# Attention and gated feed-forward on one core: where the projection weights are split, and who adds the output projection

## The reference

```python
h = _layernorm(x) * (1 + ca) + sa
qkv = (h @ W_qkv + b_qkv).reshape(b, l, H, 3 * DK).transpose(0, 2, 1, 3)
Q, K, V = jnp.split(qkv, 3, axis=-1)
scores = jnp.einsum('bhqd,bhkd->bhqk', Q, K) / np.sqrt(DK)
out = jnp.einsum('bhqk,bhkv->bhqv', softmax(scores), V)
x = x + ga * (out.transpose(0, 2, 1, 3).reshape(b, l, H * DK) @ W_fc + b_fc)
```

## Time and profile before

| | us |
|---|---|
| median of 3 runs | 1827.69 |
| lowest and highest run | 1825.25 and 1830.28 |
| the profiled execution, and its span | 1822.86 and 1821.4 |
| PE busy | 1644.4 (90%) |
| DVE busy | 1345.1 (74%) |
| POOL busy | 1130.2 (62%) |
| ACT busy | 829.1 (46%) |
| DMA queue 1 | 6.2% of 16 engines' span |

### The profile page before, as it was taken

The page is one execution under the profiler, slowest core; times in us unless marked ns, Lnnn a source line. Parts: engine busy times, 40 slices in busy tenths (PEclk is TensorE's granted clock), DMA queues, the critical chain, the costliest instruction groups (busy, mean ns, idle before and its releaser), DMA issues. The chain is left out here.

```text
span 1821.4 us, 29000 instructions
## 1 busy us (share of the span) xinstructions
PE 1644.4 (90%) x9675; PEld 900.1 (49%) x9675; DVE 1345.1 (74%) x2143; ACT 829.1 (46%) x1144; POOL 1130.2 (62%) x519
## 2 busy tenths in 40 slices
PE   4789999999999999999999999999999999945996
PEld 3444444444444444444444444444445444434886
DVE  5678777777777777777777777777777777587887
ACT  3344444444444444444444444444444444325874
POOL 3366766776766667667676666766776766720134
PEclk8899999999999999999999999999999999968999
DMA  2000000000000000000000000000000001000010
GB/s 87 18 18 18 18 18 17 17 17 17 17 17 17 17 17 1 16 17 17 17 17 17 17 17 17 17 17 17 17 17 17 17 13 49 1 24 24 30 36 29
DMA packets 31040, 37.07 MB, mean 20 GB/s; under 512 B 2174, under 2 KB 25243, under 8 KB 31003
## 3 DMA queue, kind: packets, MB, share of 16 engines
q1 hardware_dynamic: 30848, 36.58, 6.2%
q10 hardware_dynamic: 154, 0.03, 0.0%
HBM read 14.58 MB, written 2.10 MB: 9 GB/s over the span
## 5 line engine op out<-in xcount | busy, mean ns | idle before, releaser
L511 POOL TENSOR_TENSOR ACC<-ACC,PR 128x1024 f32<-128x1024 f32 x382 | 908.4, 2378 | 345.4 <-ACT PR L548 325.8
L548 ACT ACTIVATE PR<-ps_s 128x1024 f32<-128x1024 f32 x512 | 501.1, 1024 | 525.9 <-PE ps_s L754 504.7
L586 DVE TENSOR_REDUCE NMH<-ps_mx 128x2 f32<-128x1024 f32 x507 | 617.6, 1218 | 151.7 <-PE ps_mx L734 148.4
L764 PE MATMUL ps_o<-PR,V 128*64 128x512 f32 x2048 | 507.6, 614 | 4.4 <-ACT PR L548 1.1
L734 PE MATMUL ps_mx<-KHI,QHI 64*128 64x512 f32 x1014 | 234.5, 457 | 60.0 <-DVE NMH L586 60.0
L622 DVE RECIPROCAL SUM<-SUM 128x128 f32<-128x128 f32 x256 | 240.4, 941 | 6.4 <-ACT SUM L539 6.4
L764 PEld LDWEIGHTS ps_o<-PR,V 128*64 128x64 f32 x2048 | 106.1, 135 | 272.4 <-ACT PR L548 252.6
L511 POOL TENSOR_TENSOR ACC<-PR 128x1024 f32<-128x1024 f32 x64 | 150.8, 2356 | 143.0 <-ACT PR L548 143.0
L748 PE MATMUL ps_s<-QHI,KHI 64*128 64x512 f32 x1024 | 210.6, 406 | 17.6 <-DVE QLO L600 16.3
L734 PEld LDWEIGHTS ps_mx<-KHI,QHI 64*128 64x128 f32 x1014 | 95.4, 184 | 255.3 <-DVE NMH L586 161.1
L750 PE MATMUL ps_s<-QLO,KHI 64*128 64x512 f32 x1024 | 203.9, 391 | 0.0
(11 more groups left out here) (192 smaller groups left out, 1722.2 us busy)
## 6 DMA issues: line engine op xcount, KB each, us to landing
hcur<-hT SPq DMA_DIRECT2D x32, 512.0 KB, 3.3
Wraw<-in_L_attn_W_qkv SPq DMA_DIRECT2D x32, 192.0 KB, 3.0
x<-in_L_attn_X SPq DMA_DIRECT2D x4, 512.0 KB, 5.2
Wfc<-in_L_attn_W_fc SPq DMA_DIRECT2D x32, 64.0 KB, 2.5
hT<-in_L_attn_X SPq DMA_DIRECT2D x4, 512.0 KB, 6.3
out<-e_res SPq DMA_DIRECT2D x7, 256.0 KB, 2.3
e_hTs<-hT_hi SPq DMA_DIRECT2D x6, 256.0 KB, 2.3
e_hTs<-hT_lo SPq DMA_DIRECT2D x6, 256.0 KB, 2.4
```

The source lines that it names most:

```text
L511: G.tensor_tensor(ACC[:, ch, :, :], a, PR[:, t, :, :], ALU.add).then_inc(added, 1)
L548: A.activation(PR[:, t, :, :], ps_s[:, i:i + 2, :], ACT.Exp, scale=SCALE).then_inc(exp_done, 1)
L586: D.tensor_reduce(NMH[:, ch, i, kc, :], banks, AX, ALU.max, negate=True).then_inc(mx_red, 1)
L764: last = T.matmul(ps_o[half(h), ch, :], V[:, u, t, half(h)], PR[:, t, h, :], start=(t == 0), stop=(t == 7))
```

## The change

Three things change.

1. All of W_qkv is loaded in the setup stage (`Wall`, 1.5 MB) and its Q and K parts are split there once, ScalarE making `Wall_hi` and GpSimd `Wall_lo`. Each pair copies its slices of both by DMA from SBUF to SBUF into `Wqk`; V's part comes from memory as before, into `Wv`. Whi and Wlo are gone from the pairs.
2. `UNITS` has one q or k projection in each even phase instead of three in phase 2 and one in phase 6, always in bank 2; V's units move from phases 0 and 6 to 2 and 6, in bank 3. With them the reciprocals move a step, and O is computed at the end of phases 3 and 7, behind the join (`NORMALISE`). VectorE handles the units of a phase in reverse order.
3. The output projection is copied out of its bank by ScalarE (`FCS`) and added to attnT by GpSimd, after the second addition of the next half. The last pair's is still added by VectorE.

```diff
+            sp.dma_start(g.Wall[:, :, :, :, :], g.W_qkv.rearrange("e (p h t d) -> e p h t d", h=2, t=3, d=64)).then_inc(s_wall, 16)
...
             run_pairs(pool, GROUPS, body)
+            pool.wait_ge(s_whi, 2)
+            for ty in range(2):
+                nc.gpsimd.tensor_tensor(g.Wall_lo[:, :, ty, :, :], g.Wall[:, :, :, ty, :], g.Wall_hi[:, :, ty, :, :].bitcast(F32),
+                                        ALU.subtract)
...
+            act.wait_ge(s_wall, 16)
+            for ty in range(2):
+                A.activation(g.Wall_hi[:, :, ty, :, :], g.Wall[:, :, :, ty, :], ACT.Copy).then_inc(s_whi, 1)
...
-        UNITS = {0: (("rows", 0, 0, 0), ("v", 1, 0, 1), ("fc", -1, 0, 2)),
-                 2: (("k", 1, 0, 0), ("k", 1, 1, 2), ("q", 1, 0, 3)),
-                 4: (("rows", 0, 1, 0), ("fc", -1, 1, 2)),
-                 6: (("q", 1, 1, 0), ("v", 1, 1, 2))}
+        UNITS = {0: (("k", 1, 0, 2), ("rows", 0, 0, 0), ("fc", -1, 0, 3)),
+                 2: (("k", 1, 1, 2), ("v", 1, 0, 3)),
+                 4: (("q", 1, 0, 2), ("rows", 0, 1, 0), ("fc", -1, 1, 3)),
+                 6: (("q", 1, 1, 2), ("v", 1, 1, 3))}
...
+                wait(sp, q_proj, 2 * m - 2)
+                p = m % PAIRS
+                at_p = slice(p, p + 1) if isinstance(p, int) else ds(p, 1)
+                for part, w in enumerate((g.Wall_hi, g.Wall_lo)):
+                    sp.dma_start(Wqk[:, u, part, :, :, :].bitcast(F32), w[:, at_p, :, :, :].bitcast(F32)).then_inc(wqk_in[u], 16)
                 wait(sp, v_proj, 2 * m - 2)
...
+                        if t == 2 and has(n - 1):
+                            pool.wait_ge(fc_copied, 2 * (n - 1) + ch + 1)
+                            wait(pool, fc_added, 2 * (n - 1) + ch)
+                            cols = batch_cols(n - 1, ch)
+                            G.tensor_tensor(g.attnT[:, cols], g.attnT[:, cols], FCS[:, :], ALU.add).then_inc(fc_added, 1)
...
-                A.activation(Whi[:, :, :, :].rearrange("p t h d -> p h t d"), Wraw[:, u, :, 0:2, :], ACT.Copy).then_inc(w_hi, 1)
...
+                elif kind == "fc":
+                    act.wait_ge(fc_mm, 2 * m + ch + 1)
+                    wait(act, fc_added, 2 * m + ch)
+                    A.activation(FCS[:, :], ps_w, ACT.Copy).then_inc(fc_copied, 1)
...
-                        if b == 0 and j == 0 and has(n + 1):
-                            split_w(n + 1, 1 - u)
...
-                pe.wait_ge({"k": k_lo, "q": q_lo, "v": v_copied, "rows": neg_rows, "fc": fc_added}[kind], 2 * m + ch + 1)
+                pe.wait_ge({"k": k_lo, "q": q_lo, "v": v_copied, "rows": neg_rows, "fc": fc_copied}[kind], 2 * m + ch + 1)
...
                 read_out("v", 0, 1)
                 pe.wait_ge(s_init, 4)
+                pe.wait_ge(mx_red, 8)
```

More of the change, by code:

```diff
@@ L110, in build @@
             g.hT_lo = two.enter_context(nc.sbuf_tensor("hT_lo", [P, B * L], F32R))
+            g.Wall = two.enter_context(nc.sbuf_tensor("Wall", [P, 8, 2, 3, 64], F32))
+            g.Wall_hi = two.enter_context(nc.sbuf_tensor("Wall_hi", [P, 8, 2, 2, 64], F32R))
+            g.Wall_lo = two.enter_context(nc.sbuf_tensor("Wall_lo", [P, 8, 2, 2, 64], F32R))
             setup_stage(nc, g)
@@ L159, in setup_stage @@
         s_h, s_hi, s_lo = sem("s_h"), sem("s_hi"), sem("s_lo")
+        s_wall, s_whi = sem("s_wall"), sem("s_whi")
         xv = g.X.rearrange("b l e -> (b l) e").rearrange("(t p) e -> p t e", p=P)
@@ L360, in attention_stage @@
         ACC = sb("ACC", [P, 2, 2, 512])
-        Wraw = sb("Wraw", [P, 2, 2, 3, 64])
-        Whi = sb("Whi", [P, 2, 2, 64], F32R)
-        Wlo = sb("Wlo", [P, 2, 2, 64], F32R)
+        Wv = sb("Wv", [P, 2, 2, 64])
+        Wqk = sb("Wqk", [P, 2, 2, 2, 2, 64], F32R)
+        FCS = sb("FCS", [P, 512])
         bias = sb("bias", [P, 2, 2])
@@ L379, in attention_stage @@
         s_mask = sem("a_mask")
-        wraw_in, hcur_in, wfc_in = [sem("wraw_in0"), sem("wraw_in1")], sem("hcur_in"), [sem("wfc_in0"), sem("wfc_in1")]
+        wv_in, wqk_in, wfc_in = ([sem("wv_in0"), sem("wv_in1")], [sem("wqk_in0"), sem("wqk_in1")],
+                                 [sem("wfc_in0"), sem("wfc_in1")])
+        hcur_in = sem("hcur_in")
         scored, pv_done, mx_done = sem("scored"), sem("pv_done"), sem("mx_done")
@@ L517, in _, with copy_bias @@
             A = nc.scalar
-            def split_w(m, u):
+            def copy_bias(m, u):
+                wait(act, q_lo, 2 * m - 2)
                 A.activation(bias[:, u, 0:1], g.vecT[:, col(C_BQ, m)], ACT.Copy)
-                A.activation(bias[:, u, 1:2], g.vecT[:, col(C_BK, m)], ACT.Copy)
-                wait(act, wraw_in[u], (m // 2 + 1) * 16)
-                wait(act, q_proj, 2 * m)
-                A.activation(Whi[:, :, :, :].rearrange("p t h d -> p h t d"), Wraw[:, u, :, 0:2, :], ACT.Copy).then_inc(w_hi, 1)
+                A.activation(bias[:, u, 1:2], g.vecT[:, col(C_BK, m)], ACT.Copy).then_inc(s_bias, 1)
             def unit(kind, m, u, ch, ps_w):
@@ L530, in unit @@
                     act.wait_ge(proj, 2 * m + ch + 1)
+                    act.wait_ge(s_bias, m + 1)
                     A.activation(X[:, u, q], ps_w, ACT.Identity, bias=bias[:, u, ty:ty + 1]).then_inc(hi, 1)
@@ L550, in first @@
             def first():
-                split_w(0, 0)
-                act.wait_ge(w_hi, 1)
+                copy_bias(0, 0)
                 for kind, ch, ps_w in FIRST_UNITS:
                     unit(kind, 0, 0, ch, ps_w)
+                copy_bias(1, 1)
             def pair(n, u):
@@ L561, in pair @@
                     exponents(n, 2 * b + 1)
-                    if b == 0 and has(n + 1):
-                        split_w(n + 1, 1 - u)
+                    if b == 7 and has(n + 2):
+                        copy_bias(n + 2, u)
                     if b in SUMS and has(n + SUMS[b][0]):
@@ L574, in _ @@
             D = nc.vector
[L576 to L579, removed]
             def reduce_max(m, u, ch, i, kc, count, banks=ps_mx[:, :, :]):
@@ L613, in invert, with normalise @@
             def invert(m, ch, part):
[L615 to L622, removed]
+                q = slice(part * P, part * P + P)
+                dve.wait_ge(sums_in, 2 * m + ch + 1)
+                D.reciprocal(SUM[:, q], SUM[:, q]).then_inc(recip, 1)
+            def normalise(m, ch):
+                dve.wait_ge(recip, 4 * (2 * m + ch + 1))
+                wait(dve, fc_mm, 2 * m + ch)
+                D.tensor_tensor(O[:, :], ps_o[:, ch, :], SUM[:, :], ALU.mult).then_inc(o_norm, 1)
             def first():
-                split_w(0, 0)
                 for kind, ch, ps_w in FIRST_UNITS:
@@ L635, in pair @@
                 for b in range(8):
-                    for kind, m, v, ch, bank in units_of(n, u, b):
-                        unit(kind, m, v, ch, ps_s[:, bank, :])
+                    for kind, m, v, ch, bank in reversed(units_of(n, u, b)):
+                        if kind != "fc":
+                            unit(kind, m, v, ch, ps_s[:, bank, :])
                     for j in range(2):
@@ L650, in pair @@
                         join_maxima(n + 1, 0)
+                    if b in NORMALISE and has(n + NORMALISE[b][0]):
+                        normalise(n + NORMALISE[b][0], NORMALISE[b][1])
                     if isinstance(n, int) and n == 1 and b < 6:
@@ L678, in last @@
                 unit("fc", NP - 1, 1, 0, ps_s[:, 0, :])
-                for part in (0, 1, 2, 3, "O"):
+                for part in range(4):
                     invert(NP - 1, 1, part)
+                normalise(NP - 1, 1)
                 unit("fc", NP - 1, 1, 1, ps_s[:, 1, :])
@@ L692, in unit @@
                     ty = 0 if kind == "q" else 1
-                    pe.wait_ge(w_lo, m + 1)
+                    pe.wait_ge(wqk_in[u], 32 * (m // 2 + 1))
                     hi, lo = g.hT_hi[:, batch_cols(m, ch)], g.hT_lo[:, batch_cols(m, ch)]
-                    wh, wl = flat(Whi[:, ty, :, :]), flat(Wlo[:, ty, :, :])
+                    wh, wl = flat(Wqk[:, u, 0, ty, :, :]), flat(Wqk[:, u, 1, ty, :, :])
                     T.matmul(ps_w, wh, hi, start=True, stop=False)
@@ L700, in unit @@
                     pe.wait_ge(hcur_in, 16 * (m + 1))
-                    pe.wait_ge(wraw_in[u], 16 * (m // 2 + 1))
+                    pe.wait_ge(wv_in[u], 16 * (m // 2 + 1))
                     for i in range(4):
                         t = 4 * ch + i
-                        last = T.matmul(ps_w[:, i * P:(i + 1) * P], hcur[:, t * P:(t + 1) * P], Wraw[:, u, :, 2, :],
+                        last = T.matmul(ps_w[:, i * P:(i + 1) * P], hcur[:, t * P:(t + 1) * P], Wv[:, u, :, :],
                                         start=True, stop=True)
```

18 lines of the change are left out of this document (8 added, 10 removed).

## The result

| | before | after |
|---|---|---|
| median, us | 1827.17 (4 runs) | 1738.03 (4 runs) |
| lowest and highest | 1825.25, 1830.28 | 1737.47, 1738.61 |
| profiled execution and span | 1822.86, 1821.4 | 1737.47, 1735.8 |

The ratio is 0.9506, 95% interval 0.9495 to 0.9518: 89 us faster. The forecast was 1745 with a range of 1733 to 1770.

What follows compares the result with a forecast made beforehand. TensorE was taken to bound the kernel, its gaps being what could be won. From 1822.9 us, less 89.0 for 31 pairs, plus 5.3 setup and 1.2 end, came 1740.4, or 1745 on the median's scale; range 1733 to 1770.

Steps and rivals of the forecast that it cites:

- What bounds the kernel: Long middle: TensorE sets the pace, busy 378.8 of 400 us; the missing 5% can be won.
- The sum over phases: One pair's phases added without gaps: 2.87 us saved a pair, from 47.80 to 44.9 us.
- Wlo's place: Phase 0: Wlo before the second reduction leaves TensorE idle 1.77 us before phase 1's first maxima.
- the whole table: Read-out gaps of phases 2 and 6, removed by the new units table: 1.1 us a pair.
- Wlo waits for GpSimd: Phase 0: Wlo takes 2.19 us instead of 0.43 because it waits for GpSimd's addition, not for its arithmetic.
- 31 pairs of equal gain: Pairs 0 to 30 each save 2.87 us, together 89.0 us.
- the 2 us of loss: Pair 1: gate rows with two SBUF inputs wait for GpSimd's additions, some 2 us once in the kernel.
- Setup and end: First attention matmul 5.3 us later through the setup split; GpSimd's last addition chain 1.2 us longer.
- A: Whole kernel: gaps go and nothing new comes, 1745 us, own range 1737 to 1752; chance 75%.
- C: First pairs, where TensorE also waits: more comes back than counted, 1730 to 1737 us; chance 4%.
- B: Six places in a pair: reduction or QHI late by 0.2 to 0.3 us, 1760, at most 1801; chance 18%.
- D: GpSimd's addition to attnT sets the pace, binding from 6.0 us an addition; 1852 us at 7.7; chance 2%.

Runs made afterwards that it cites:

- experiment 1: The kernel before with one line moved, so VectorE computes Wlo behind the second reduction of phase 0: 1768.7 us, ratio 0.9684.
- experiment 2: The kernel before with Wlo behind the second reduction and phase 6's q and v in banks 2 and 3: 1749.0 us, ratio 0.9581.
- experiment 4: The changed kernel with the old UNITS table and VectorE's order in a phase put back: 1776.7 us, ratio 0.9727.
- experiment 3: The kernel before with only Q's half of Wlo computed for pairs 1 to 31: 1819.0 us in one run.
- Experiments 9 and 10: The changed kernel: again, 1738.2 us; weights split earlier in setup, 1731.5; that plus two more last additions on VectorE, 1729.6.
- experiment 5: The changed kernel with VectorE adding the output projection straight from its bank, without FCS copy or GpSimd addition: 1751.6 us, ratio 0.9586.
- experiment 8: The changed kernel with four unused GpSimd additions of 128x512 before each addition to attnT: 1828.1 us in one run.
- experiment 6: The kernel before with Wlo moved, VectorE's order changed and a new units table, no setup split or FCS: 1756.4 us, ratio 0.9608.

## Why the prediction came out as it did

**What bounds the kernel.** Right. In the middle TensorE's gaps were what could be won, and they are gone: 398.45 of 400.

**The sum over phases.** Right to 0.01 us: 44.93 measured, 47.80 - 2.87 = 44.93 forecast. Experiments 1, 2 and 4 show the terms apart: 1.86 for Wlo's place, 0.52 for phase 6, 1.29 for the whole table (forecast 1.77, 0.52, 1.1).

**Wlo waits for GpSimd, and its place makes that costly.** Shown by experiments 3 and 1.

**31 pairs of equal gain.** The term that was mis-sized. I took pairs 0, 1 and 30 like the others. From transpose to transpose pair 0 went from 50.96 us (60.16 to 111.12) to 45.43 (65.34 to 110.77): 5.5 less, not 2.9, of which 1.5 are owed to the first transpose coming later behind a projection (18.8 us after the first matmul instead of 17.3). Pair 1 carries six instructions of VectorE for the gate rows, four of them with two SBUF inputs; the prediction took all for such. The kernel before, one of them and TensorE in pair 1:

```profile
133.17 2.44 DVE L664 TENSOR_SCALAR mod_rep<-mod_rep 128x512 f32<-128x512 f32 x1
...
136.79 0.51 PE L734 MATMUL ps_mx<-KHI,QHI 64*128 64x512 f32 x2 [1.56 <-DVE NMH L586]
141.66 0.50 PE L748 MATMUL ps_s<-QHI,KHI 64*128 64x512 f32 x2 [0.94 <-DVE QN L604]
```

The first gap stands behind an instruction with only one SBUF input. It took 2.44 us, where another such instruction of the same width took 0.36 in the changed kernel (at 122.22), and it ended 0.28 us after a GpSimd addition (132.94 to 135.33), as Wlo does. So not only two inputs make VectorE wait. After, no such gap is left in pair 1, though VectorE's gate rows are still blocked, for instance this one, which took 0.68 in the kernel before:

```profile
115.58 2.79 DVE L683 SCALAR_TENSOR_TENSOR mod_rep<-mod_rep 128x512 f32<-128x512 f32 x1
```

The rule of the Trainium skill (SBUF — State Buffer, "Who interferes with whom") holds on this one (2.79 against 0.68 us), but the 2 us of loss that I drew from it were not there: pair 1 now takes 45.7 us from transpose to transpose (110.77 to 156.49) where it took 51.7 (111.12 to 162.86), 6.0 less. VectorE now has room enough to be blocked without TensorE waiting. From the first matmul to the end of pair 1 the two pairs gave 10.0 us where 5.7 were counted, 4.3 more. Pair 30 went from 48.49 to 44.72 us, 0.9 more than counted; the pairs between gave 2.87 each.

**Setup and end.** 5.3 us forecast and 3.7 measured at the first matmul; 1.2 forecast and 1.2 measured at the end (from pair 31's first transpose to the feed-forward stage 50.6 us before and 51.8 after). Experiments 9 and 10 show that both losses were real and could be had back.

**The feed-forward stage.** I took it as unchanged, and its code is. In the profiled executions it lasts 220.9 us before (1600.47 to the end) and 224.7 after (1511.12 to the end). Windows of its first 100 us, before and then after:

```profile
1600.47:1700.47 100.00, 61.75 (x336) 49.51 (x337) 80.33 (x389) 51.27 (x95) 13.89 (x14) 0.81 0.09 27
```

```profile
1511.12:1611.12 100.00, 62.83 (x303) 50.94 (x304) 78.56 (x370) 46.98 (x87) 13.98 (x14) 0.73 0.07 22
```

The granted clock, a mean over stretches at either of its two levels, is 0.73 of full speed instead of 0.81, and fewer instructions got done (370 against 389 on VectorE). In all 13 profiles this stage has the same code and took 221 to 227 us: 220.8 or 220.9 in the four where this clock was 0.81, 226.9 to 227.1 in the three where it was 0.67 to 0.70, 222 to 225 in those between. So time and clock of this stage go together in these profiles; what sets the clock stays open.

**Where the 7 us between 1745 and 1738 come from.** They come from the sum. Up to the feed-forward stage the changed kernel is 89.4 us shorter (1600.47 against 1511.12) where 82.5 were forecast: 4.3 more in pairs 0 and 1, 0.9 in pair 30, 1.6 in the setup. The profiled spans differ by only 85.6 us because the feed-forward stage was 3.8 us longer in the profile of after, at the lower clock. The 4.8 us that I added to get from the profile to the median were right: the profile of before had that stage at its shortest, and its time lay 4.3 us under the kernel's median, while that of after lay at its own.

**The rivals.** A held, at its lower edge. What pulled it there is what C named: the first pairs, where TensorE also waited. I gave that 4%, and the 4.3 us of it are real; with 1738.0 the time only just stayed out of C's range. B (late reads) did not come: the slacks were 0.2 to 0.4 us, and experiment 5 shows what 0.69 more costs, 0.39 a pair. D did not come either; it named the right engine for experiment 8, and the wrong point. I let GpSimd bind at 6.0 us an addition, from its busy time; the ring gives 1.3 + 2.9 = 4.2. And I would have looked for a GpSimd without idle time, while it set the pace with 1.4 us idle in each ring.

## What to carry to other kernels

An instruction that is blocked by another engine costs what stands behind it in its own queue, so look at the order first: one moved line was worth 58 us, two bank numbers some 16 to 20 more, and the new stage, copies and buffers the last 12 or so. When TensorE is the bound and the pattern is periodic, add the phases of one period without their gaps, and then walk each phase to see that the other engines can follow. Here that gave the period to a hundredth of a microsecond; in experiment 6, where the expectation left out what two KLO in phase 2 cost, it missed by 0.4 to 0.7 us. The first and last periods need a look of their own. The room of an engine is not its idle time: it is what the ring that it is in leaves free. GpSimd, with 2.9 us to spare, cost 90 us when it was given 4.4.

## What the runs showed of the hardware

- VectorE's subtraction of 128x256 took 0.43 us alone and 2.19 beside GpSimd's addition of 128x1024; with half the columns it still took 2.06.
- What was held ended a time after the addition that goes with its own width: 0.15 us with 128 columns, 0.28 with 256, and 0.54 to 0.56 with 512 (the gate rows with two SBUF inputs, such as the one at 115.58, ending at 118.37 after an addition that ends at 117.82). That is as if all of its work came after the wait.
- A VectorE instruction with one SBUF input (128x512, 32 bits) was held too: 2.44 us, ending 0.28 us after the addition, against 0.36 for one that was not held.
- GpSimd's addition of 128x512 took 1.28 us in the median as attnT + FCS and 1.04 as FCS + FCS into JUNK (four in a row 4.39). Inputs and output differ between the two; which of them makes the difference was not tested.
- The same code of the feed-forward stage took 220.8 us at a mean granted clock of 0.81 over its first 100 us and 227.1 us at 0.67.
